# An adaLN block with linear attention and a top-2 mixture of experts: counts by tree sums, early bias products, expert weights kept in SBUF

## The reference, cut to what matters

```
mod = (silu(c) @ wmod).reshape(8, 6, 1, 128)          # sa, ca, ga, sb, cb, gb
ga, gb = sign * max(abs, 0.25)
h = layernorm(x) * (1 + ca) + sa
x = x + ga * attention(h)      # q, k, v, gate: 128x128; RoPE; linear attention over 8 heads;
                               # depthwise convolution of v with 5 taps; gating; output product
h = layernorm(x) * (1 + cb) + sb
logits = h @ Wg + bg;  probs = softmax(logits / 5)     # 8 experts
top 2 -> gates, normalised to sum 1
out_e = gelu(h @ W1[e] + b1[e]) @ W2[e] + b2[e]        # 128 -> 256 -> 128
x = x + gb * sum over e of gates[e] * out_e
```

## Time and profile before

| | |
|---|---|
| median of 3 runs | 496.46 us (495.05 to 497.1) |
| the profiled execution | 495.53 us, span from first to last instruction 493.7 us |
| TensorE (PE) | busy 419.6 us (85%), 2824 instructions, mean granted clock 0.913 |
| its weight loads (PEld) | busy 351.4 us (71%), 2824 |
| VectorE (DVE) | busy 311.7 us (63%), 1094 |
| ScalarE (ACT) | busy 300.1 us (61%), 805 |
| GpSimd (POOL) | busy 301.4 us (61%), 293 |
| DMA | 85.54 MB, mean 173 GB/s |

### The profile page before, as it was taken

One profiled execution on the slowest core, in us unless ns is written; L12 is line 12 of the kernel. 1 busy time (PEld: TensorE's weight loads), 2 busy tenths in 40 slices (PEclk: granted clock), 3 DMA queues, 4 the chain that ended last, 5 costly groups with the idle time before them and its releaser, 6 DMA issues.

```text
span 493.7 us, 9831 instructions
## 1 busy us (share of the span) xinstructions
PE 419.6 (85%) x2824; PEld 351.4 (71%) x2824; DVE 311.7 (63%) x1094; ACT 300.1 (61%) x805; POOL 301.4 (61%) x293
## 2 busy tenths in 40 slices
PE   2578788699999999999999999989997999699410
PEld 2354475388889889887988798869887889499200
DVE  3387899585768577959787789866870712222423
ACT  1454553468689777758686878585737677376100
POOL 0320138527524887766787878877787777747571
PEclk9997968788999998899899999998998999889755
DMA  7900402384576663757275946664667689768412
GB/s 234 314 27 2 170 6 74 109 292 136 168 222 201 203 195 91 217 159 235 76 216 175 286 138 179 198 194 117 199 199 224 181 264 299 253 191 244 124 51 65
DMA packets 72263, 85.54 MB, mean 173 GB/s; under 512 B 9930, under 2 KB 53074, under 8 KB 71954
## 3 DMA queue, kind: packets, MB, share of 16 engines
q1 hardware_dynamic: 56674, 54.95, 37.1%
q0 software_dynamic: 8192, 16.79, 11.8%
q10 hardware_dynamic: 7344, 13.17, 7.3%
HBM read 53.40 MB, written 31.47 MB: 172 GB/s over the span
## 4 chain that ended last, share of the span: by engine, by line
PE 42%; POOL 27%; issue 9%; DVE 9%; ACT 6%; DMA 4%; POOLq 0%; ACTq 0%
POOL og L673 14%; POOL x_sort L663 10%; PE ps_o L488 8%; PE ps_hid L474 8%; PE bank L366 4%; ACT xn L516 4%; POOL rstd L639 3%; PE bank L400 3%; DVE stats L684 2%; DMA og<-o_sort,slots 2%; PE bank L435 2%; PE bank L379 2%; PE bank L394 2%; PE ps_x L462 2%; PE ps_z L495 2%
## 5 line engine op out<-in xcount | busy, mean ns | idle before, releaser
L663 POOL DMA_INDIRECT x_sort<-xn,slots x128 | 137.0, 1070 | 44.8 <-issue 35.7
L673 POOL DMA_INDIRECT og<-o_sort,slots x128 | 128.0, 1000 | 47.9 <-issue 38.2
L601 ACT ACTIVATE hid<-ps_hid,w 128x128 f32<-128x128 f32 x368 | 105.8, 374 | 40.3 <-PE ps_hid L474 35.3
L488 PE MATMUL ps_o<-w_f,hid 128*128 x736 | 102.8, 285 | 4.9 <-ACT o_s L609 3.4
L474 PEld LDWEIGHTS ps_hid<-xs_t,w 128*128 128x128 f32 x736 | 93.8, 196 | 12.7 <-issue 7.5
L474 PE MATMUL ps_hid<-xs_t,w 128*128 128x128 f32 x736 | 101.8, 282 | 0.8 <-ACT xs_t L591 0.8
L488 PEld LDWEIGHTS ps_o<-w_f,hid 128*128 128x128 f32 x736 | 93.1, 198 | 11.2 <-issue 10.9
L639 POOL TENSOR_TENSOR rstd<-var_eps,minus_half 128x8 f32<-128x8 f32 x16 | 29.1, 1817 | 86.1 <-DVE var_eps L694 85.9
L892 DVE SCALAR_TENSOR_TENSOR u<-og,gate,ps_z 128x128 f32<-128x128 f32 x64 | 21.7, 341 | 53.6 <-DMA og<-o_sort,slots 42.1
L366 PE MATMUL bank<-wqkvg_f,h 128*128 128x384 f32 x128 | 50.8, 519 | 4.3 <-ACT v L541 2.9
L836 DVE TENSOR_TENSOR qk_cos<-bank,rope_f 128x256 f32<-128x256 f32 x64 | 26.7, 417 | 32.0 <-PE bank L366 31.9
(11 more groups left out here) (127 smaller groups left out, 648.8 us busy)
## 6 DMA issues: line engine op xcount, KB each, us to landing
w<-in_w_all SPq DMA_DIRECT2D x184, 129.0 KB, 3.5
o_sort<-o_s ACTq DMA_DIRECT2D x48, 256.0 KB
xg<-x_sort SPq DMA_DIRECT2D x40, 256.0 KB, 4.2
x_sort<-zero SPq DMA_DIRECT2D x24, 256.0 KB, 4.1
xs<-in_x SPq DMA_DIRECT2D x8, 512.0 KB, 4.0
out<-y SPq DMA_DIRECT2D x16, 256.0 KB
x_sort<-xn,slots POOLq DMA_INDIRECT x128
og<-o_sort,slots POOLq DMA_INDIRECT x128
```

What stands on the lines that cost most here:

```text
L488: last = pe.matmul(ps_o[:, m % GROUP, :], hid[k % HID_RING][:, m % 2, h, :], second.rearrange("p e f -> p (e f)"), start=(h == 0), stop=(h ...
L601: last = act.activation(hid[k % HID_RING][:, m % 2, h, :], ps_hid[k % 2][:, m % 2, h, :], ACT.Gelu, bias=w[:, HID + h:HID + h + 1])
L663: pool.indirect_dma_start(x_sort[b % SORTS], bass.IndirectOffsetOnAxis(ap=at, axis=0), xn2[i][:, n, :], None).then_inc(s_scat[b % SORTS], 16)
L673: pool.indirect_dma_start(og[:, k, n, :], None, o_sort[i], bass.IndirectOffsetOnAxis(ap=at, axis=0)).then_inc(s_gat[n], 16)
```

## The change

- Routing: `choose` gets three more steps. `chosen` is padded with zero tiles in front, and adding it to itself shifted by one, two and four tiles gives `chosen_sum`, the running sum over tiles. "prefix" is two products with the last tile's sums (`before`, `every`). In "place", one tile's base row is formed first and then added to `chosen_sum` for all tiles: one step more.
- Biases: "b2" moves from the experts' stages to the routing (its tick is behind "gT"). After each product VectorE multiplies the half by gb into `bias` and adds that to `x1`. The combination no longer adds `ps_z`: its first step is a `tensor_scalar` product. The gates' transpose has 2 buffers for 5.
- Start: x of batch 0 is SP's first load; VectorE takes batch 0's first statistics before the modulation; ScalarE waits for the modulation at its first "xT" only.
- Weights: `w_f` holds both layers and the first bias of all experts (514 columns each for 256). "w" is ScalarE's stage: it reads the owners and copies 258 columns from `w_f` into one of 8 buffers `w1`. SP no longer loads them. The owner's buffer is protected by `s_w1`, now one count.
- All ticks in `BEGIN`, `BEGIN_EXPERTS` and `AT` are new, so the order in every queue changes.

```diff
-BEGIN = [0, 225, 446, 673, 892, 1123, 1346, 1576]
-BEGIN_EXPERTS = [0, 240, 484, 730, 981, 1217, 1444, 1688]
+BEGIN = [0, 225, 441, 658, 875, 1090, 1307, 1522]
+BEGIN_EXPERTS = [0, 216, 434, 648, 865, 1081, 1305, 1525]
...
-W_RING, XG_RING, XS_RING, HID_RING, O_RING = 15, 3, 2, 2, 2
-w_f = sb("w_f", [P, E, HH * D])
+W_RING, XG_RING, XS_RING, HID_RING, O_RING = 8, 3, 2, 2, 2
+w_f = sb("w_f", [P, E, WCOLS])
...
 # SP
-elif kind == "w":
...
-            sp.dma_start(wmod_f, wmod).then_inc(s_w["mod"], 16)
             stage(0, "load", 0)
+            sp.dma_start(wmod_f, wmod).then_inc(s_w["mod"], 16)
 # PE, prefix
-                    pe.matmul(pos, before[:, :], chosen[:, :], start=True, stop=False)
-                    for k in range(1, J + 1):
-                        last = pe.matmul(pos[:, k * E:], every[:, :], chosen[:, 0:(J + 1 - k) * E], ...)
+                    for k, sums in enumerate((before, every)):
+                        last = pe.matmul(of("prefix", b)[:, k * E:(k + 1) * E], sums[:, :], chosen_sum[:, J * E:], ...)
 # PE, b2
-                    if 2 * b + n >= 1:
-                        pe.wait_ge(s_first, J * b + n * JC)
+                    if b + n >= 1:
+                        pe.wait_ge(s_bias, CH * b + n)
 # ACT
+                    if b == 0 and n == 0:            # xT
+                        act.wait_ge(s_mod, 3)
+                elif kind == "w":
+                    k = nth(b, n)
+                    if n == 0:
+                        act.wait_ge(s_route, ROUTE * (b + 1))
...
+                    if n % GROUP == 0:
+                        whose[:] = owners(mybir.EngineType.Activation, b, n // GROUP)
+                    if k >= W_RING:
+                        old_b, old_t = divmod(k - W_RING, TILES)
+                        act.wait_ge(s_gelu, couple(old_b, old_t // 2) + 1)
+                    first = w_f[:, bass.ds(whose[n % GROUP], 1), 0:HID + HH]
+                    act.activation(w1[k % W_RING][:, :], first.rearrange(...), ACT.Copy).then_inc(s_w1, 1)
-            act.wait_ge(s_mod, 3)                    # before the list
 # DVE, choose
-step(b, 12, dve.tensor_tensor(chosen[:, 0:J * E], hot[:, 0, :], hot[:, 1, :], ALU.add))
+step(b, 12, dve.tensor_tensor(chosen[:, E:], hot[:, 0, :], hot[:, 1, :], ALU.add))
+step(b, 13, dve.tensor_tensor(by_two[:, 2 * E:], chosen[:, E:], chosen[:, 0:J * E], ALU.add))
+step(b, 14, dve.tensor_tensor(by_four[:, 4 * E:], by_two[:, 2 * E:], by_two[:, 0:J * E], ALU.add))
+step(b, CHOSEN, dve.tensor_tensor(chosen_sum[:, E:], by_four[:, 4 * E:], by_four[:, 0:J * E], ALU.add))
 # DVE, b2
+                    dve.wait_ge(s_b2, CH * b + n + 1)
...
+                    dve.tensor_tensor(bias[:, :, :], ps_z[:, :]..., gb[:, b, :]..., ALU.mult).then_inc(s_bias, 1)
+                    dve.wait_ge(s_bias, CH * b + n + 1)
+                    dve.tensor_tensor(x1[b % LAG][:, half, :], x1[b % LAG][:, half, :], bias[:, :, :], ALU.add)...
 # DVE, comb
-                    dve.scalar_tensor_tensor(u[:, n, :], og[:, 0, n, :], g[:, 0, n:n + 1],
-                                             ps_z[:, n % JC * D:(n % JC + 1) * D], ALU.mult, ALU.add)...
+                    dve.tensor_scalar(u[:, n, :], og[:, 0, n, :], g[:, 0, n:n + 1], None, ALU.mult)...
 # DVE, start
+            for c in range(CH):
+                stage(0, "stat1", c)
             dve.wait_ge(s_mod_ps, 1)
```

More of the change, by code:

```diff
@@ L86, in owner_before, with adaln_moe_kernel @@
     return ORDER[k] if k >= 0 else None
-def adaln_moe_kernel(nc, x, wqkvg, wo, wmod, c_t, lepe, w_route, b_route, w1_all, w2_all, b2, rope, consts, out):
+def adaln_moe_kernel(nc, x, wqkvg, wo, wmod, c_t, lepe, w_route, b_route, w_all, b2, rope, consts, out):
     with ExitStack() as ctx:
@@ L164, in adaln_moe_kernel @@
         gates = sb("gates", [P, J, E])
-        gates_t = [sb(f"gates_t{i}", [J * E, P]) for i in range(LAG)]
+        gates_t = [sb(f"gates_t{i}", [J * E, P]) for i in range(2)]
+        bias = sb("bias", [P, JC, D])
         gate2 = [sb(f"gate2_{i}", [P, TOP, J]) for i in range(LAG)]
         over = sb("over", [P, E, E])
-        n_tiles, base, ends = sb("n_tiles", [P, E]), sb("base", [P, E]), sb("ends", [P, E])
+        n_tiles, base, row, ends = (sb(n, [P, E]) for n in ("n_tiles", "base", "row", "ends"))
         place = sb("place", [P, J * E])
@@ L220, in adaln_moe_kernel @@
         s_scat = [sem(f"s_scat{i}") for i in range(SORTS)]
-        s_w1 = [sem(f"s_w1_{i}") for i in range(W_RING)]
+        s_w1 = sem("s_w1")
         s_xg = [sem(f"s_xg{i}") for i in range(XG_RING)]
@@ L335, in _ @@
             sp.dma_start(gb[:, :, :], gab_dram[:, D:2 * D].partition_broadcast(P)).then_inc(s_gab, 16)
-            sp.dma_start(w_f[:, :, :], w2_all).then_inc(s_w["experts"], 16)
+            sp.dma_start(w_f[:, :, :], w_all.rearrange("e p f -> p e f")).then_inc(s_w["experts"], 16)
             sp.wait_ge(s_set, SETS)
@@ L442, in stage @@
                     bank_free("prefix", b)
-                    pos = of("prefix", b)[:, 0:(J + 1) * E]
-                    pe.matmul(pos, before[:, :], chosen[:, :], start=True, stop=False)
-                    for k in range(1, J + 1):
-                        last = pe.matmul(pos[:, k * E:], every[:, :], chosen[:, 0:(J + 1 - k) * E], start=False,
-                                         stop=(k == J))
+                    for k, sums in enumerate((before, every)):
+                        last = pe.matmul(of("prefix", b)[:, k * E:(k + 1) * E], sums[:, :], chosen_sum[:, J * E:], start=True,
+                                         stop=True)
                     last.then_inc(s_pos, 1)
@@ L483, in stage @@
                         e = whose[g][m % GROUP]
-                        if nth(b, m) == 0:
-                            pe.wait_ge(s_w["experts"], 16)
                         for h in range(HH):
-                            second = w_f[:, bass.ds(e, 1), h * D:(h + 1) * D]
+                            second = w_f[:, bass.ds(e, 1), HID + HH + h * D:HID + HH + (h + 1) * D]
                             last = pe.matmul(ps_o[:, m % GROUP, :], hid[k % HID_RING][:, m % 2, h, :],
@@ L492, in stage @@
                     pe.wait_ge(s_gt, b + 1)
-                    if 2 * b + n >= 1:
-                        pe.wait_ge(s_first, J * b + n * JC)
-                    pe.matmul(ps_z[:, :], gates_t[b % LAG][:, :], b2_f[:, n * CT:(n + 1) * CT], start=True, stop=True)\
+                    if b + n >= 1:
+                        pe.wait_ge(s_bias, CH * b + n)
+                    pe.matmul(ps_z[:, :], gates_t[i][:, :], b2_f[:, n * CT:(n + 1) * CT], start=True, stop=True)\
                         .then_inc(s_b2, 1)
@@ L762, in place_and_soften @@
                 put_done(4)
[L763 to L764 removed]
+                put(dve.scalar_tensor_tensor(row[:, :], base[:, :], float(P), prefix[:, 0:E], ALU.mult, ALU.add))
                 soft_done(4)
@@ L883, in stage @@
                     place_and_soften(b)
+                elif kind == "b2":
+                    dve.wait_ge(s_b2, CH * b + n + 1)
+                    if b + n >= 1:
+                        dve.wait_ge(s_x1b, CH * b + n)
+                    dve.tensor_tensor(bias[:, :, :], ps_z[:, :].rearrange("p (j d) -> p j d", d=D),
+                                      gb[:, b, :].unsqueeze(1).to_broadcast([P, JC, D]), ALU.mult).then_inc(s_bias, 1)
+                    dve.wait_ge(s_bias, CH * b + n + 1)
+                    dve.tensor_tensor(x1[b % LAG][:, half, :], x1[b % LAG][:, half, :], bias[:, :, :], ALU.add).then_inc(s_x1b, 1)
                 elif kind == "comb":
-                    c = n // JC
                     dve.wait_ge(s_gat[n], 16 * TOP * (b + 1))
-                    if n % JC == 0:
-                        dve.wait_ge(s_b2, CH * b + c + 1)
-                        if b >= 1:
-                            dve.wait_ge(s_y, CH * (b - 1) + c + 1)
+                    if n % JC == 0 and b >= 1:
+                        dve.wait_ge(s_y, CH * (b - 1) + n // JC + 1)
                     g = gate2[b % LAG]
-                    dve.scalar_tensor_tensor(u[:, n, :], og[:, 0, n, :], g[:, 0, n:n + 1],
-                                             ps_z[:, n % JC * D:(n % JC + 1) * D], ALU.mult, ALU.add).then_inc(s_first, 1)
+                    dve.tensor_scalar(u[:, n, :], og[:, 0, n, :], g[:, 0, n:n + 1], None, ALU.mult).then_inc(s_first, 1)
                     for j in (n - 1, n)[n % JC == 0:1 + (n % JC == JC - 1)]:
```

78 lines of the change are left out of this document (39 added, 39 removed), and 38 rows, old and new, of the table AT.

## The result

The changed kernel takes 503.0 us (median of 4 runs, 499.8 to 504.49), the kernel before beside it 495.75 us (493.26 to 497.1): ratio 1.0143, interval 1.0077 to 1.021. It is slower; the forecast was 487.5. The profiled execution took 502.21 us, its span is 500.4. All ratios in this document are of runs in the faster of the chip's two states; the traces of e3_sp_loads, e4_old_order_sp_loads and e7_old_experts are of runs in the slower one.

What follows compares the result with a forecast made beforehand. TensorE and GpSimd were both taken as full in the middle. Expert stream -4.0 - 4.7 - 6.8 + 5 = -10.5, GpSimd -4.0 - 4.5 - 3.5 + 3 = -9.0; the later, GpSimd, gave 487.5 us, range 477 to 505.

Steps and rivals of the forecast that it cites:

- the first term of the *Sum: Fill: x loaded first and early statistics bring batch 0's transposes forward 2.4 to 5.5 us; 4.0 taken for both streams.
- VectorE's 2.8 us "once or twice": Fill: VectorE's added bias products and adds, 2.8 us a batch, are not hidden there and cost that once or twice.
- Biases early: Tail: TensorE's 4.32 us wait at a b2 product goes; VectorE's extra 2.8 us a batch is hidden, except in the fill.
- Middle: TensorE 4.7, GpSimd 4.5: Full middle: two count products for nine save TensorE 4.7 us; GpSimd gains only its 4.5 us of waiting.
- Tail: 6.8 and 3.5: Tail: early biases gain the expert stream 6.8 us; GpSimd gains 3.5, batch 6's gathers starting at 437.4 instead of 440.94.
- GpSimd held by 16 adds: 3 lost: GpSimd: indirect DMAs that meet VectorE's 16 new adds with two SBUF inputs wait for their end; 3 us lost.
- ScalarE's copies: 5 lost: Expert stream: with copies ScalarE takes 50.0 us a batch against TensorE's 49.3; 5 us lost over 7 batches.
- the first rival: ScalarE decides, at 52.1 us a batch with copies, loads and issues in the open: 500 to 510 us; chance 0.23.
- The second rival: Copies are free: ScalarE at 44.6 us a batch hides them, GpSimd hardly ever held: 482 to 484 us; chance 0.15.
- VectorE holds GpSimd: Combinations: 64 products of 128 columns each stop an indirect DMA, +13 us on GpSimd's -9.0: 500 us; chance 0.12.
- the third rival: VectorE's 64 first-combination products hold up GpSimd's indirect DMAs, whose mean would exceed 1.12 us: 500 us; chance 0.12.
- The signs of being right: Transposes before 15.2; no ps_z wait over 1 us; middle ScalarE over 85%, TensorE 95%; batch 6's gathers within 1 us.

Runs made afterwards that it cites:

- e3_sp_loads: The changed kernel in its new order, with first layers loaded by SP again (ring of 15) and no copies by ScalarE: ratio to the kernel before 0.9876.
- e4_old_order_sp_loads: The changed kernel with the order of the kernel before and first layers loaded by SP as before: ratio to the kernel before 0.9938.
- e7_old_experts: The changed kernel with new ticks for attention and routing, but old ticks and begins for the experts: ratio to the kernel before 1.0774.
- e8_start_only: The kernel before with the early start alone (x first, first statistics ahead of the modulation, ScalarE's wait moved): ratio to the kernel before 0.9951.
- e5: The changed kernel with prefix and place moved behind the next batch's key-value product (ticks 368 to 390): ratio to the kernel before 1.0216.
- e10: The changed kernel with the next batch's kv products and first convolution step ahead of the prefix again: ratio to the kernel before 1.0255.
- e13_twelve_first: The changed kernel with, in three batches, the last 4 of 16 scatters behind the next batch's powers on GpSimd: ratio to the kernel before 0.9707.
- e2_copies_only: The kernel before with only the first layers copied by ScalarE (ring of 8) instead of loaded by SP: ratio to the kernel before 1.0045.
- e13b_twelve_first: The changed kernel with the last 4 scatters behind the next batch's powers in three batches, run again in more rounds: ratio to the kernel before 0.9704.
- e11_bias_later: The changed kernel with the biases' three operations at later ticks, behind the next batch's numerators: ratio to the kernel before 0.9846.

## Why the prediction was wrong

**The step that failed is the first term of the *Sum*, -4.0 for both streams.** "The transposes move from 17.53 to 12 to 15.1" came true: 12.71, 4.8 us early. But the sum carries that gain to the end as if everything behind it kept its order. In the old order it is kept: e8_start_only has batch 1's prefix 4.2 us early. The change also rewrites the order, and this I priced at nothing. At batch 0's second powers 1.8 us of the 4.8 were left (49.14 for 50.94). At the first scatter there was a loss of 0.8 (71.72 for 70.94); the same program, with more clock from 50 to 60 us, has that scatter at 69.36 and 69.25 elsewhere, a gain of 1.6. At batch 1's powers the loss is 6.25.

The table would have shown it. Before, "pow2" of batch 1 is at 225 + 264 = 489, just ahead of batch 0's scat_6 at 490; after, at 225 + 300 = 525, behind scat_7 at 489. That is 4 scatters, one every 1.25 us by my own reading of the earlier trace rows, so 5.0 us in each batch of the fill whose powers the queue holds, against a gain of 4.0. The powers start at the later of two things: their data (14.4 us after the first scatter before, 18.5 after) and the end of the scatters ahead (16.0 to 17.3 us for 12, 21.3 to 23.1 for 16; in e5 and e10 the data come later still). In the old and in the new kernel it is the queue; e13_twelve_first makes it the data, at 18.8. In the changed kernel's first trace the data were ready at 90.25 and the powers started at 94.47, so the queue held them for 4.2 of the 6.25 us.

**VectorE's 2.8 us "once or twice" was left out of the sum.** The later data are this term, which the section *Biases early* names for the fill and the *Sum* leaves at nothing. With the biases moved back, the data come 2.9 us sooner behind the first scatter (15.6 for 18.5), most of the 4.1 by which the new order delays them. It takes both moves, twelve scatters ahead and later biases, to have the old fill back, and no run has both with all else new.

**Middle: TensorE 4.7, GpSimd 4.5.** Half right: TensorE gained 2.5 us in the middle. GpSimd idled 10.2 us for others from 178 to 435 (6.2 in the earlier trace rows), nearly all of it for VectorE's statistics and placing, while TensorE was busy 225.9 of 234 us. So GpSimd was not the bound that I made of it; that it was TensorE, late from the fill, is my reading of these shares.

**Tail: 6.8 and 3.5.** The wait at ps_z is gone (18.3 us in the earlier trace rows, now 0.0), and batch 6's gathers start right behind batch 5's last combination, as forecast. But in place of 440.94 they start at

```profile
448.52 0.94 POOL L680 DMA_INDIRECT og<-o_sort,slots  x1 [3.17 <-DVE u L914]
...
471.43 0.94 POOL L680 DMA_INDIRECT og<-o_sort,slots  x1 [3.23 <-DVE u L914]
```

because batch 7's scatters, 13.4 us late (last 426.72 for 413.37), now stand among batch 5's gathers on GpSimd. TensorE was 5.0 us behind at 412 (7.5 less 2.5) and 4.9 at its last second layer: in the tail it gained nothing. It stood 3.00 us at 450.96 for a Gelu that was queued on ScalarE behind an o_sort issue, which waited for the same combination: the wait moved from TensorE to ScalarE.

**GpSimd held by 16 adds: 3 lost.** The size is near, the cause is not shown: from 178 to 435 us scatters went from 1049 to 1101 ns, 86 of them 4.5 us; gathers fell from 1011 to 984, 2.4 us back. Of the 256 indirect DMAs of the trace, 21 run beside one of the adds, on average 1043 ns, where the 49 beside no instruction of VectorE take 959; that is under 2 us for the adds.

**ScalarE's copies: 5 lost.** Nothing was lost where I looked: over the whole span TensorE's second layers waited 6.3 us for Gelus, 3.00 of it at the one place in the tail. No run shows it for the total (e2_copies_only leaves room for 0 to 0.9%). A copy lasts 443 ns, two together 0.74, so one follows the other by 0.31, as worked out. ScalarE is busy 349.8 / 8 = 43.7 us a batch and 85% of the middle; the 50.0 took loads and issues to be in the open. Both the first rival's mechanism and its point, 51.5 us a batch, were missed: 503 us lies in its span of 500 to 510, by another cause. The second rival's condition (44.6 or less) was met, its time was not.

**VectorE holds GpSimd.** The gathers did not get longer (984 ns for 1011), and one that ran beside such a product took its usual 0.94 us, so the third rival falls:

```profile
441.91 0.94 POOL L680 DMA_INDIRECT og<-o_sort,slots  x1 [0.30 <-issue]
...
442.07 0.28 DVE L910 TENSOR_SCALAR u<-og,gate 128x128 f32<-128x128 f32 x1 [3.32 <-DMA og<-o_sort,slots]
```

The Trainium skill says in "SBUF — State Buffer" ("Who interferes with whom") that a `tensor_scalar` can enter a two-port mode and then shuts GpSimd out. Nothing of that showed here with 64 of them, 285 ns each; whether they ran in that mode no run shows.

**The signs of being right.** All four came true: transposes at 12.71, no wait at ps_z, ScalarE at 85% and TensorE at 96.5% in the middle, batch 6's gathers 0.8 us behind batch 5's last combination. None of them looks at the fill behind the first transposes, which is where the time went.

**What stays open.** The changed kernel is 1.4% slower than the kernel before on the first chip and 1.4 to 1.5% faster in the two later comparisons, both on one other chip (only the second interval lies below 1). So no experiment repeats the slowdown that it is to explain. The traces agree on the fill to about 120 us; behind that they differ by the stands at "remote", whose cause no run shows. It is shown that GpSimd's order costs 4 to 5 us at batch 1's prefix, in either kernel. Not shown is how much of the 6.7 us its mending would give back on the first chip; at batch 1's powers it is at most the 4.2 us that the queue held them. e13b_twelve_first shows that a lower clock can eat the gain before it reaches the prefix.

## What to carry to other kernels

When a change comes with a new written-out order, price the order as an edit of its own: for each engine, list what stands ahead of each instruction on the path in the fill, before and after, and multiply by the row's pace. A short instruction that starts the next batch's chain belongs ahead of bulk work in the same queue; here four indirect DMAs ahead of one power cost as much as the early start brought. A gain at one of two waits shows only when the other is gone: the later biases brought the data forward, and the queue hid it. And count instructions done by a given time: it says where a kernel falls behind, which busy shares do not.

## What was not expected of the hardware

One program takes 496 us on one chip and 659 to 675 on others. The changed kernel, traced on both kinds, has much the same first 120 us and then stands of up to 37 us at "remote". A small change of order moved the time there by 1.5% (e13_twelve_first against its control) to 4% (e10_kv_ahead against e11_bias_later), so a ratio taken on such a chip is no forecast for another. And TensorE's clock in the first batch is not the same from run to run: granted 0.69 from 50 to 60 us in the changed kernel's first trace and 1.00 in both later ones, with the first scatter at 71.72, 69.36 and 69.25 us.
